# A batched attention and feed-forward kernel: another bank and slot for one transpose, another place for a second

## What is computed

```python
x = x + attn_a(layernorm(x))   # 16 heads of 8, rotary, per-head layer norm, softmax over 256 keys
x = x + ffn(layernorm(x))      # token shift; sigmoid(xr @ Wr.T) * (relu(xk @ Wk.T)**2 @ Wv.T)
x = x + attn_b(layernorm(x))   # window attention with memory, one gradient step on an MLP, gates
x = x + ffn(layernorm(x))
```

## Time and profile before

| what | value |
|---|---|
| time, median of 3 runs | 1403.64 us (1403.26 to 1405.39) |
| span of the profiled execution, first to last instruction | 1400.9 us |
| what lies around the span, median less span | 2.7 us |
| TensorE busy | 1322.9 us (94%) |
| VectorE busy | 1129.1 us (81%) |
| ScalarE busy | 931.6 us (66%) |
| GpSimd busy | 489.8 us (35%) |
| mean granted TensorE clock | 0.988 |

### The profile page before, as it was taken

The page is one execution under the profiler, slowest core; times in us unless marked ns, Lnnn a source line. Parts: engine busy times, 40 slices in busy tenths (PEclk is TensorE's granted clock), DMA queues, the critical chain, the costliest instruction groups (busy, mean ns, idle before and its releaser), DMA issues.

```text
span 1400.9 us, 33350 instructions
## 1 busy us (share of the span) xinstructions
PE 1322.9 (94%) x10635; PEld 858.3 (61%) x10635; DVE 1129.1 (81%) x2909; ACT 931.6 (66%) x2570; POOL 489.8 (35%) x815
## 2 busy tenths in 40 slices
PE   7889999999999999887899999999999998999996
PEld 5445555555555555544566666666666665888885
DVE  5788989889988989875777788877887775787876
ACT  2278888888888888875566665666566663555563
POOL 4446666666666666432001000000001000223232
PEclk9899999999999999999999999999999999999998
DMA  2222232222333332200001010100001001233231
GB/s 78 75 74 79 78 81 76 77 72 77 80 85 99 101 83 78 74 23 16 27 24 35 24 48 25 31 28 24 24 24 34 21 16 32 79 84 88 82 85 31
DMA packets 101967, 79.65 MB, mean 57 GB/s; under 512 B 13780, under 2 KB 95124, under 8 KB 101796
## 3 DMA queue, kind: packets, MB, share of 16 engines
q1 hardware_dynamic: 100820, 76.99, 19.8%
q10 hardware_dynamic: 976, 0.54, 0.2%
HBM read 49.70 MB, written 27.79 MB: 55 GB/s over the span
## 4 chain that ended last, share of the span: by engine, by line
PE 49%; issue 1%; DVE 1%; ACT 1%; POOL 0%; POOLq 0%; DVEq 0%; ACTq 0%
PE b_g L1357 4%; PE b_psD L1309 4%; PE b_psZ L1386 4%; PE b_psZ L1320 4%; PE d_psO L1912 4%; PE b_g L1370 4%; PE d_psH L1904 4%; PE b_psR L1363 3%; PE b_psM L1419 2%; PE b_psR L1379 2%; PE b_psL L1348 2%; PE b_psD L1409 2%; PE b_psM L1431 1%; PE b_psM L1439 1%; PE d_psG L1930 1%
## 5 line engine op out<-in xcount | busy, mean ns | idle before, releaser
L783 DVE TENSOR_REDUCE a_MX<-a_psS 128x4 f32<-128x1024 f32 x256 | 312.6, 1221 | 39.9 <-PE a_psS L296 39.7
L586 ACT ACTIVATE a_PT<-a_psE 128x512 f32<-128x512 f32 x504 | 274.1, 603 | 54.2 <-PE a_psE L313 53.9
L1769 POOL TENSOR_TENSOR b_SWB<-b_b2col,b_SW 128x128 f32<-128x128 f32 x65 | 25.9, 399 | 329.7 <-ACT b_SW L1503 329.7
L327 PE MATMUL a_psV<-a_PT,a_VX 128*32 128x256 f32 x2048 | 137.9, 387 | 0.2 <-ACT a_PT L586 0.2
L296 PE MATMUL a_psS<-a_KS,a_QS 48*128 48x256 f16 x1024 | 101.4, 276 | 23.6 <-DVE a_MX L783 21.0
L313 PE MATMUL a_psE<-a_QS,a_KS 50*128 50x256 bf16 x1008 | 97.6, 270 | 1.1 <-ACT a_PT L586 1.1
L1539 ACT ACTIVATE b_PR<-b_psL,b_mx 128x128 f32<-128x128 f32 x260 | 92.3, 365 | 3.0 <-DVE b_mx L1661 2.8
L296 PEld LDWEIGHTS a_psS<-a_KS,a_QS 48*128 48x128 bf16 x1024 | 30.2, 94 | 95.7 <-DVE a_MX L783 64.2
L1533 ACT ACTIVATE b_HT<-b_psR 128x512 f32<-128x512 f32 x65 | 38.8, 597 | 73.3 <-PE b_psR L1363 73.3
L327 PEld LDWEIGHTS a_psV<-a_PT,a_VX 128*32 128x32 f32 x2048 | 53.7, 109 | 51.5 <-issue 29.1
L1637 DVE SCALAR_TENSOR_TENSOR b_DZ<-b_U,b_psD 128x512 f32<-128x512 f32 x65 | 44.7, 688 | 43.7 <-PE b_psD L1309 42.7
(11 more groups left out here) (294 smaller groups left out, 3479.2 us busy)
## 6 DMA issues: line engine op xcount, KB each, us to landing
a_KS<-kparts SPq DMA_DIRECT2D x63, 192.0 KB
a_QS<-qparts SPq DMA_DIRECT2D x126, 96.0 KB
qparts<-a_QP SPq DMA_DIRECT2D x64, 96.0 KB, 2.2
a_X<-x_in SPq DMA_DIRECT2D x32, 128.0 KB, 2.3
kparts<-a_KP SPq DMA_DIRECT2D x64, 64.0 KB, 2.1
x<-a_X SPq DMA_DIRECT2D x32, 128.0 KB, 1.8
b_X<-x SPq DMA_DIRECT2D x32, 128.0 KB, 2.2
zT<-b_XT SPq DMA_DIRECT2D x32, 128.0 KB, 1.7
```

Of the source, the lines that this page charges most:

```text
L327: mm = nc.tensor.matmul(psV[32 * h:32 * h + 32, 0:T], VX[:, b % UV, kt, at:at + 32], PT[:, gg, kt, h, :], start=(gg == 0 and kt == 0), sto ...
L586: nc.scalar.activation(PT[:, g % 2, :, h + s, :], shifted_bank(b, p, s), ACT.Exp).then_inc(S["exp"], 1)
L783: nc.vector.reduce_max(MX[:, b % 2, :].rearrange("q (s n) -> q s n", s=2)[:, :, 2 * p:2 * p + 2], psS[:], AX.X).then_inc(S["max"], 1)
```

## The change

Three things, all in phase a:

- z_t(b) for b of 3 and more writes psC columns 256 to 511 instead of psA columns 0 to 255, and stands in slot 5 behind on_t instead of slot 4 behind pv(c-4, 1), on TensorE. It waits for on(b-6) and v(b-1) instead of square(b-1) and centred(b-1). The copy to ZT1 on ScalarE reads the new place and moves to the head of slot 5, behind the exponentials of that slot.
- on_t and ffn_kr no longer wait for that copy (zT).
- max_t(c-3) stands ahead of pv(c-5, 3) in slot 0 instead of behind it, with the same waits.

No operation is added or removed.

```diff
--- before.py
+++ after.py
@@ -342,7 +342,7 @@
 
         def zt_bank(b):
 
-            return psC if b < 3 else psA
+            return psC[:, 0:T] if b < 3 else psC[:, T:2 * T]
 
         def z_t(b):
             wait(pe, "z", b)
@@ -351,8 +351,8 @@
             if b == 2:
                 wait(pe, "v", b - 1)
             if b >= 3:
-                wait(pe, "square", b - 1)
-                wait(pe, "centred", b - 1)
+                wait(pe, "on", b - 6)
+                wait(pe, "v", b - 1)
             for t in range(NT):
                 mm = nc.tensor.transpose(zt_bank(b)[:, t * P:(t + 1) * P], Z[:, t, :], ident[:])
             mm.then_inc(S["zT_ps"], 1)
@@ -420,7 +420,6 @@
 
         def on_t(b):
             wait(pe, "on", b)
-            wait(pe, "zT", b + 6)
             if b < B - 1:
                 wait(pe, "fzT", b - 1, per=4)
             for t in range(NT):
@@ -452,7 +451,6 @@
                 pe.wait_ge(S["prep"], 3)
             wait(pe, "square", b + 6)
             wait(pe, "centred", b + 6)
-            wait(pe, "zT", b + 7)
             if b >= B - 6:
                 wait(pe, "gv", b - 1)
             wait(pe, "mixed", b, per=2, done=1)
@@ -479,10 +477,10 @@
                 if p == 0:
                     if on(c):
                         proj_q(c)
+                    if on(c - 3):
+                        max_t(c - 3)
                     if on(c - 5):
                         pv(c - 5, 3)
-                    if on(c - 3):
-                        max_t(c - 3)
                 if p == 1:
                     if on(c):
                         centre(c)
@@ -499,11 +497,11 @@
                 if p == 4:
                     if on(c - 4):
                         pv(c - 4, 1)
-                    if on(c + 1):
-                        z_t(c + 1)
                 if p == 5:
                     if on(c - 5):
                         on_t(c - 5)
+                    if on(c + 1):
+                        z_t(c + 1)
                     if on(c - 6):
                         ffn_kr(c - 6)
                 if p == 6:
@@ -601,7 +599,7 @@
         def z_t(b):
             wait(act, "zT_ps", b)
             wait(act, "q_ps", b - 1)
-            nc.scalar.activation(ZT1[:], (psC if b < 3 else psA)[:, 0:T], ACT.Copy).then_inc(S["zT"], 1)
+            nc.scalar.activation(ZT1[:], psC[:, 0:T] if b < 3 else psC[:, T:2 * T], ACT.Copy).then_inc(S["zT"], 1)
 
         def proj_v(b):
             wait(act, "vp_ps", b)
```

## The result

The change makes the kernel slower, by about half of what was forecast: 1407.82 us (median of 13 runs, 1405.28 to 1408.64) against 1404.34 us (13 runs, 1402.46 to 1406.93), ratio 1.0021 with a 95% interval of 1.0011 to 1.0031, that is +1.5 to +4.4 us (3.5 us between the medians) where +6.8 was forecast. In a later set of runs it was 1406.06 against 1403.74 us, ratio 1.0014 (1.0004 to 1.0023). The span of its profiled execution is 1406.0 us against 1400.9. Every run on record with both figures took 1.7 to 1.9 us more than its own span, so the 2.7 us of the table of before are these and 0.9 us by which the profiled execution was quicker than the median of three. One run of a later kernel (max_t in the other bank, with more filler) took 2135.3 us at a mean granted clock of 0.554; it is left out of that kernel's median.

The account below looks back on a forecast made before the run. Bound: TensorE and VectorE chains meeting without slack at slot 1's row maximum. 27 x 0.27 = +7.3 us and 25 x -0.02 = -0.5 us gave +6.8 us, span 1407.7, plus 2.7: 1410.4 us; range 1404.5 to 1414.5.

Parts of the forecast that it names:

- The hold of max_t: Slot 0, TensorE: max_t waits for the copy into VX (L617), delaying slot 1's scores by +0.27 us an iteration.
- no slack between them: Start of slot 1's row maximum: TensorE's scores and VectorE's sine meet at 311.90, so delayed scores delay it.
- The sum of +4.4 us: Slot 0 alternative: pv's first weight load passes the held max_t, hiding 0.09 us; total +4.4 instead of +6.8 us.
- VectorE carries it on: Slots 1 to 4: VectorE's chain passes the +0.27 us delay on to the scores of slot 5.
- the next late thing was L658: Slot 5: without the ZT1 wait, on_t is held by ScalarE's last fzT copy until 302.45, gaining 0.27 us.
- ScalarE's room: Slot 5: the ZT1 copy behind the exponentials has about 0.1 us of room before spread; cost 0.
- slower still: Rival, slots 5 and 6: the ZT1 copy pushes spread by 0.15 us an iteration; +10.6 us, 1414.2 us; chance 0.13.
- The count: Phase a: max_t's cost charged for 27 iterations (c = 5 to 31), z_t's term for 25 (c = 6 to 30).
- z_t in slot 5 ... -0.02 us: Slot 5, TensorE: on_t's gain less z_t's added transposes nets -0.02 us an iteration, 25 x -0.02 = -0.5 us.
- nothing measurable: Rival, slot 1: hidden slack absorbs 0.1 us an iteration, with -0.12 in slot 5; +1.6 us, 1405.2 us; chance 0.14.

Follow-up runs that it names:

- max_t in the other bank, with more filler: Changed kernel, max_t writing a bank proj_v doesn't use, two unread filler matmuls a slot instead of one in iterations 2 and 3: 1398.23 us.
- max_t alone: Kernel before with max_t ahead of pv(c-5, 3) and nothing else: 1411.17 us against 1403.74, ratio 1.0040.
- the one without the wait: Changed kernel, max_t writing a bank proj_v doesn't use, without the wait for v in all but the last three batches: 1397.07 us against 1406.06.
- two other pairs of kernels: z_t in slot 5 against slot 4 in iterations 2 to 4 only: kernel before 1401.99 against 1404.86 us, kernel with only z_t moved 1397.42 against 1401.58.
- z_t alone: Changed kernel with max_t back behind pv(c-5, 3): 1397.76 us, ratio 0.9950 against before; run again, 1397.42 us, ratio 0.9951.

## Why the prediction came out wrong in size

**The hold of max_t: right, and 0.02 to 0.03 us too small.** 0.79 us from L370 to max_t was forecast, 0.84 measured: the latency from the end of L615 to the held step is 0.14 to 0.15 us in all 25 iterations, not the 0.10 taken from on_t. The steps behind it are 0.20 and 1.00 us, and slot 0 grew by 0.29 us instead of 0.27. The run with max_t alone (+0.28 an iteration) and the one without the wait (2.79 us) show that this is the cause and all of it. The step "no slack between them" was all but right: the row maximum could have started 0.06 us earlier. The end of sine at 311.91 wasn't what it waited for, since VectorE's records overlap (sine itself starts at 311.05, and cosine, L806, ends at 310.26 + 0.88 = 311.14). The sum of +4.4 us, for a weight load of pv that passes the held max_t, lies nearer to the measured time, but not for its reason: that load starts 0.20 us behind the start of max_t in all 25 iterations.

**VectorE carries it on: right.** Slots 1 to 4 have the lengths of before (2.96, 1.87, 2.05, 1.80 us), so nothing was given back there.

**Slot 5: the next late thing was L658, as said, but the term was too small.** -0.07 us instead of -0.02, from three distances. on_t came 0.05 us later behind shifted than forecast (0.46 against 0.41), again for a latency of 0.14 us. ffn_kr follows z_t by 0.22 us, not by the 0.25 us of on_t's own pair, which comes out of a hold. And the second part of ffn_kr follows the first by 0.43 us, where I had carried over 0.50. Together +0.05 - 0.03 - 0.07 = -0.05 us. The last of them lies inside the first part of ffn_kr and not in a wait for the second mix of GpSimd, which was in time as forecast: its two matmuls take 0.60 us (L457) where they took 0.66 (L459). Their first weight load starts 0.11 us ahead of the first matmul now, and started 0.04 us ahead of it, right behind on_t:

```profile
302.93 0.30 PEld L459 LDWEIGHTS a_psA<-a_FX,a_wk_t 128*128 128x128 f32 x2
```

z_t now stands between on_t and ffn_kr, and ffn_kr has one wait less. That the late load is the reason for the 0.07 us is read from the rows, and which of the two lets it come early no run isolates.

**ScalarE's room: right.** spread starts 0.04 us after the last Newton step; slot 6 is 2.65 us as before. The rival "slower still" had no part in it.

**The count: too generous, which hid the hold's size.** 27 iterations were charged in full. In iteration 5 slot 0 grows by 0.18 us and slot 1 shrinks by 0.12 (3.03 and 2.46 against 2.85 and 2.58); iteration 31 gives back 0.12 of its 0.29 in the same way. So the two at the edges cost some 0.2 us and not 0.54, and the hold comes to 6.99 + 0.2 = 7.2 us in the run of max_t alone, against 7.3 forecast. z_t's part comes to -2.07 us against -0.5: a steady -0.07 us, and more in single iterations (in 27 slot 5 took 2.46 us before and takes 2.33). The 25 iterations from 6 to 30 cost 5.05 us where 25 x 0.25 = 6.25 was forecast, and with the two at the edges it is some 5.3 us of the 6.8.

**The failed steps: "z_t in slot 5 ... -0.02 us", and all else kept as it was.** The first is a term of the sum that was too small: 25 x -0.02 = -0.5 us was forecast and -2.07 us measured, which takes the sum from 6.8 to 5.3 us. The second is a term that stood at nothing without a reason: the sum carried the 1400.9 us of one execution along as a constant, and with it the granted clock. The runs show a median clock of 0.988 for the change and 0.986 for before, and 5 to 6 us between the kernels at an equal clock where the medians differ by 3.5, so some 2 us of the cost were made up by the clock. Where in the kernel the change gains it is open. Its early z_t was the suspect, and in two other pairs of kernels that slot moved the median by 2.9 and 4.2 us; in the changed kernel it didn't, and in both of its traces iterations 2 to 4 took longer than before. The page gave a mean clock of 0.988; I didn't ask what the kernel pays in its stretches of low clock, nor which of the moved steps stand in them. The rival "nothing measurable" (+1.6 us) lies inside the measured interval, but not for its reason: nothing was absorbed in slot 1.

**A better version** falls out of this: z_t moved and max_t left behind pv, 1397.4 to 1397.8 us, or max_t ahead of pv but in the bank that proj_v doesn't use, 1397.07 us. Both beat both kernels, before by 6 to 7 us and the change by 8 to 10 us. Part of that is again granted clock: at a mean clock of 0.989 the middle runs took 1401.13 us (before, 4 runs) and 1397.42 us (z_t alone, 3 runs). Their intervals (0.9935 to 0.9965 and 0.9932 to 0.9960) don't tell the two apart; in the 25 iterations they took 454.79 and 453.29 us.

## What to carry to other kernels

Before moving a step forward in an in-order list, look up when each of its waits is met, not only whether it is met today: a wait that was free by 0.83 us at the old place held four steps by 0.29 us an iteration at the new one. When a step moves between slots, price it in the fill of the pipeline as well as in its steady state: there TensorE has gaps, and a slot's change in three iterations moved the median by 2.9 and 4.2 us in two kernels and not at all in a third. And when two executions of one kernel differ by as much as the effect, compare runs of equal mean clock, and stretches at equal granted clock slot by slot; the steady 25 iterations repeated to 0.2 us where whole runs of one kernel spread over 10 us (1398.99 to 1409.12).

## What the runs showed of the hardware that was not expected

- The step that waits for a ScalarE copy started 0.10 us after the copy's end in one place (L427 after L604) and 0.14 to 0.15 us after it in two others (L426 after L656, L341 after L615), each in all 25 iterations from 6 to 30.
- Moving two transposes by one slot in three iterations at the start, of 32 batches' work, changed the median by 2.9 us (before) and 4.2 us (z_t alone), with the steady iterations unchanged. With the transposes in slot 4 the mean clocks of the runs were 0.982 to 0.991 and 0.983 to 0.993, in slot 5 0.985 to 0.989 and 0.989 to 0.990.
- A transpose with a 32-column operand between proj_q and the value products took less time than the same one behind them: 1.64 us from L370's counterpart to the next scores, against 1.74 us.
- Two kernels with the same steps in iterations 2 to 4 (z_t alone, and the change) took 53.4 us and 54.8 to 55.9 us for them in two traces each, at different granted clocks.
